# Products without a reader in TensorE's waits of the last group, and a slot table worked out in two parts

## The chip, the cores and the metric

One NeuronCore of a Trainium2 chip runs the whole kernel in one launch. The metric is the device time of one execution in microseconds. The trace covers the span from the first to the last instruction; the time of an execution is about 2 us longer than its span.

## The reference

Two transformer layers over 16 sequences of 128 tokens, width 192, 12 heads of 16, all in float32. Cut to what matters here:

```python
h = tok_embed(x, itok)                       # two gathered tables, layer norm, gate
h = h + L0_attn(layernorm(h))                # linear attention with cumulative sums
h = h + L0_ffn(layernorm(h))                 # 15% of tokens attend, the rest mix; then gelu(n2 @ W1) @ W2
h = h + L1_attn(layernorm(h))                # softmax attention: exp(q k^T), 12 heads per sequence
h = h + L1_ffn(layernorm(h))                 # 8 experts, the two best of each token, gelu MLP 192-768-192
```

The last line is routed: each token has two experts, and the kernel sorts the 4096 (token, expert) pairs into tiles of 128 rows that belong to one expert each. There can be up to 39 such tiles (`MT`).

## The kernel before

The 16 sequences go through in four groups of four (`G = 4`, `NG = 4`). Every engine has its program written out by hand in one order, and the engines meet only in semaphores: `w(turn, name, n)` waits until `n` steps of the stage `name` are done. TensorE works strictly in the order written.

`front(0)` does the first layer of group 0. `joint(g + 1, g)` weaves the first layer of one group with the second layer of the group before, so TensorE has two chains to draw from. `back(NG - 1)` is what is left: feed-forward, second attention and routing of the last group alone. In it TensorE has one chain only:

- the norm `ln4` (VectorE, a root on GpSimd), `n4_T` (TensorE transposes into PSUM), an evacuation on ScalarE, and then the products of `up_half`, `down_half`, `qk1_half`, `v1_half`;
- the second attention, sequence by sequence (b = 0 to 3): `logits(b)`, then VectorE's `maxima(b)`, `max_T(b)` (three transposes), VectorE's `below(b)`, `logits_T(b)`, ScalarE's `exps(b)`, `av1(b)`, `o_T(b)`, VectorE's `attend(b)`. With `wide` the even sequences live in the four PSUM banks `QC` and the odd ones in `QA`, and `logits(b)` waits for the second step of `attend(b - 2)`;
- the expert tiles. `work(k)` on TensorE is `up(k + 1)`, `x_T(k + 2)`, `down(k - 1)`. VectorE's `evacuate(k)` copies the transposed tile k + 2 (`xT_evac`), copies its expert's weights (`stage_w1`) and scales the output of tile k - 1 (`weight`). GpSimd's `add(k)` adds the 128 rows to the output by an indirect DMA; each add waits until the one before has landed. SyncE's `slot_load(k)` fetches a tile's rows, and from tile 6 on waits for the add of tile k - 6.

Which expert a tile belongs to comes from a table in SBUF. It is worked out twice on VectorE: `table(0, EARLY, NG - 1)` for the first 12 tiles from the groups before the last, and `table(EARLY, MT, NG)` for the other 27 once the last group is routed. The second is called after `evacuate(5)` and `rows_out`, in front of `evacuate(6)`. SyncE sends the last group's rows out (`base_rows(NG - 1)`, behind `rows_out`) in its queue between the slot loads of tiles 9 and 10.

`front` already has a helper `stream(n)`: n products of 32 output rows by 512 columns into a bank that nobody reads.

Of the kernel before, what the change touches and what calls it, by code (L numbers as in the profile page):

```python
# [33 lines left out]
RING = 6  # L34
# [40 lines left out]
def build(nc, a, out):  # L75
    with ExitStack() as ctx:
# [959 lines left out]
        def _(dve):  # L1036
# [448 lines left out]
            def maxima(tb, b, hf, wide=False):  # L1485
                w(tb, "lg1", b + 1)
                nc.vector.reduce_max(mx1[:, :, HD].rearrange("p (j i) -> p i j", i=4)[:, 2 * hf:2 * hf + 2, :],  # L1487
                                     sec(b, wide)[:, 2 * hf:2 * hf + 2, 0:384].rearrange("p i (j t) -> p i j t", j=3), AX.X)\
                    .then_inc(s["mx1"], 1)
# [251 lines left out]
            def back(tb):  # L1741
                ln4_half(tb, 0)
                selected_in(tb, 1)
                ln4_half(tb, 1)
                ln4_half_apply(tb, 0)
                ln4_half_apply(tb, 1)
                ffn_out(tb, 0)
                ln5_half(tb, 0)
                ln5_half_apply(tb, 0)
                ffn_out(tb, 1)  # L1750
                ln5_half(tb, 1)
                ln5_half_apply(tb, 1)
                table(0, EARLY, NG - 1)
                maxima(tb, 0, 0, True)
                maxima(tb, 0, 1, True)
                below(tb, 0, True)
                maxima(tb, 1, 0, True)
                maxima(tb, 1, 1, True)
                below(tb, 1, True)
                attend(tb, 0, True)  # L1760
                maxima(tb, 2, 0, True)
                maxima(tb, 2, 1, True)
                below(tb, 2, True)
                attend(tb, 1, True)
                maxima(tb, 3, 0, True)
                maxima(tb, 3, 1, True)
                below(tb, 3, True)
                dve.wait_ge(ld_w1, 16 * NE)
                stage_w1(0, 0)
                attend(tb, 2, True)  # L1770
                xT_evac(0, 0)
                xT_evac(1, 1)
                stage_w1(1, 1)
                attend(tb, 3, True)
                ln6_stats(tb)
                stage_w1(2, 2)
                ln6_apply(tb)
                xT_evac(2, 2)
                evacuate(1, 1, 0)
                gate_max(tb)  # L1780
                evacuate(2, 2, 0)
                top_two(tb)
                top_weights(tb)
                evacuate(3, 3, 0)
                slot_rows(tb)
                evacuate(4, 4, 0)
                evacuate(5, 5, 0)
                rows_out(tb, 0)
                rows_out(tb, 1)
                table(EARLY, MT, NG)  # L1790
                for tile in range(RING, EARLY):
                    evacuate(tile, tile % RING, tile // RING)

            done = [0]
# [7 lines left out]
                dve.wait_ge(route, n)  # L1802

            def table(lo, hi, g):
                m = hi - lo
                dve.wait_ge(s["pos"], g * PER["pos"])
                n = r_step(STT(cnt[:, 0, :], con("iota8"), -float(REGION), first_row[:, 0, :], ALU.mult, ALU.add))
                r_wait(n)
                n = r_step(TS(cnt_i[:, 0, :], cnt[:, 0, :], 127.0 if lo else 0.0, None, ALU.add))
                r_wait(n)  # L1810
                n = r_step(TS(cnt_i[:, 1, :], cnt_i[:, 0, :], 7, None, ALU.logical_shift_right))
                r_wait(n)
                n = r_step(nc.vector.tensor_copy(cnt[:, 1, :], cnt_i[:, 1, :]))
                r_wait(n)
                if lo:
                    n = r_step(T(cnt[:, 1, :], cnt[:, 1, :], taken[:, 0:NE], ALU.subtract))
                    r_wait(n)
                n = r_step(T(upto, con("le8").rearrange("p (e k) -> p e k", e=NE), bc(cnt[:, 1, :], 1, NE), ALU.mult))
                k = r_step(TS(cnt[:, 3, :], cnt[:, 1, :], -128.0, float(REGION), ALU.mult, ALU.add))
                r_wait(n)  # L1820
                n = r_step(nc.vector.reduce_sum(cnt[:, 2, :], upto, AX.X))
                r_wait(n)
                if lo:
                    r_wait(k)
                    k = r_step(STT(cnt[:, 4, :], taken_d, 128.0, cnt[:, 3, :], ALU.mult, ALU.add))
                    n = r_step(TS(cnt[:, 2, :], cnt[:, 2, :], float(lo), None, ALU.add))
                    r_wait(n)
                else:
                    r_step(fill(upto_e[:, 0:1], 0.0))
                    n = r_step(TS(upto_e[:, 1:NE + 1], cnt[:, 2, :], float(hi), None, ALU.min))  # L1830
                    r_wait(n)
                    r_step(fill(taken[:, NE:NE + 1], 0.0))
                    n = r_step(T(taken[:, 0:NE], upto_e[:, 1:NE + 1], upto_e[:, 0:NE], ALU.subtract))
                    r_wait(n)
                    r_step(T(taken_d, taken[:, 1:NE + 1], taken[:, 0:NE], ALU.subtract))
                    r_step(TS(shift, taken[:, 0:1], 128.0, -128.0 * hi, ALU.mult, ALU.add))
                    r_wait(k)
                    k = r_step(nc.vector.tensor_copy(cnt[:, 4, :], cnt[:, 3, :]))
                at_slot = con("slot")[:, lo:hi]
                n = r_step(T(owner[:, lo:hi, :], bc(at_slot, 2, NE), bc(cnt[:, 2, :], 1, m), ALU.is_ge))  # L1840
                r_wait(k)
                r_wait(n)
                k = r_step(T(skip[:, lo:hi, :], owner[:, lo:hi, :], bc(cnt[:, 4, :], 1, m), ALU.mult))
                n = r_step(nc.vector.reduce_sum(ownf[:, lo:hi], owner[:, lo:hi, :], AX.X))
                r_wait(k)
                k = r_step(nc.vector.reduce_sum(rowf[:, lo:hi], skip[:, lo:hi, :], AX.X))
                r_wait(n)
                n = r_step(TS(own_i[:, lo:hi], ownf[:, lo:hi], float(NE - 1), None, ALU.min))
                r_wait(k)
                k = r_step(STT(skip[:, lo:hi, 0], at_slot, 128.0, rowf[:, lo:hi], ALU.mult, ALU.add))  # L1850
                r_wait(k)
                if lo:
                    k = r_step(T(skip[:, lo:hi, 0], skip[:, lo:hi, 0], shift.to_broadcast([128, m]), ALU.add))
                    r_wait(k)
                k = r_step(TS(skip[:, lo:hi, 1], skip[:, lo:hi, 0], float(NE * REGION), None, ALU.min))
                r_wait(k)
                k = r_step(nc.vector.tensor_copy(row_i[:, lo:hi], skip[:, lo:hi, 1]))
                r_wait(k)
                r_wait(n)
                n = r_step(fill(first[:, 0:1], 0.0))  # L1860
                assert n == (R_DONE if lo else R_EARLY), n
# [17 lines left out]
            def evacuate(tile, u, turn):  # L1879

                if more(tile, 2):
                    xT_evac(tile + 2, (u + 2) % RING)
                    stage_w1(tile + 2, (u + 2) % RING)
                if more(tile, -1):
                    weight(tile - 1, (u - 1) % RING)
# [10 lines left out]
        def _(pe):  # L1896
# [355 lines left out]
            def stream(n):  # L2252
                for _ in range(n):
                    mm(PC[0:32, 0, :], ident[:, 0:32], w_l0[:, 0, 0:512])

            def front(ta):
                stream(4)
                x1_T(ta, 0)
# [184 lines left out]
                attn(ta, 1)  # L2443

            def back(tb):
                n4_T(tb, 0)
                up_half(tb, 0, 0)
                up_half(tb, 1, 0)
                n4_T(tb, 1)
# [18 lines left out]
                    qk1_half(tb, n, 1)  # L2468
                v1_half(tb, 1)
                logits(tb, 0, True)  # L2470
                max_T(tb, 0, True)
                logits_T(tb, 0, True)
                logits(tb, 1, True)
                av1(tb, 0, True)
                max_T(tb, 1, True)
                logits_T(tb, 1, True)
                o_T(tb, 0, True)
                logits(tb, 2, True)
                av1(tb, 1, True)
                max_T(tb, 2, True)  # L2480
                logits_T(tb, 2, True)
                o_T(tb, 1, True)
                logits(tb, 3, True)
                av1(tb, 2, True)
                max_T(tb, 3, True)
                logits_T(tb, 3, True)
                o_T(tb, 2, True)
                av1(tb, 3, True)
                w(tb, "h_l1", 3 * 2 + 2)
                x_T(0, 0, 1)  # L2490
                o_T(tb, 3, True)
                x_T(1, 1, 1)
                w(tb, "h_l1", 3 * 3 + 2)
                pe.wait_ge(route, R_EARLY)
                up(0, 0)
# [172 lines left out]
```

## Time and profile before

| | us |
|---|---|
| median of 3 runs | 879.14 (877.9 to 880.11) |
| the profiled execution | 878.32 |
| its span | 876.3 |
| TensorE busy | 729.2 (83%) |
| VectorE busy | 520.1 (59%) |
| mean granted TensorE clock | 0.923 of full |

The profiled execution lies 0.8 us under the median and 2.0 us over its own span. [...] A float32 product is two instructions, a transpose is one.

### The profile page before, as it was taken

What the parts mean: (1) busy time and instruction counts of PE and PEld (TensorE: products, weight loads), DVE (VectorE), ACT (ScalarE), POOL (GpSimd) and SP (SyncE); (2) the same over time, 40 slices, a digit from 0 to 9 for tenths busy, and PEclk for the clock granted to TensorE, in tenths of its full rate; (3) what the DMA queues carried; (4) which work ended last, traced back from release to release, by engine and by line L of the source; (5) the groups of instructions that cost most, each with busy time, mean ns of one, the idle gap of its engine ahead of it and who ended that gap; (6) DMA issues with size and microseconds to landing.
All of it is one profiled execution on the core that took longest, in us unless ns stands there. A gap on an engine that the chain in (4) does not pass through costs nothing.

```text
span 876.3 us, 15714 instructions
## 1 busy us (share of the span) xinstructions
PE 729.2 (83%) x5548; PEld 561.7 (64%) x5549; DVE 520.1 (59%) x1766; ACT 303.9 (35%) x700; POOL 243.4 (28%) x302
## 2 busy tenths in 40 slices
PE   1888777989678998867899976868878989999993
PEld 0546465566457565656666555757756989998892
DVE  7558757873678785668877476891434553333330
ACT  0033232624333263433244344223323433333330
POOL 5332200460013246001443300142000453333332
PEclk9999989999978999998899997797956999999998
DMA  7960000000000000000122000019301233222220
GB/s 251 411 247 1 1 1 1 19 8 1 1 1 28 27 19 8 1 2 1 37 35 9 1 3 1 1 55 344 90 1 29 43 73 47 38 37 38 36 35 8
DMA packets 29894, 43.63 MB, mean 50 GB/s; under 512 B 5355, under 2 KB 24597, under 8 KB 29830
## 3 DMA queue, kind: packets, MB, share of 16 engines
q1 hardware_dynamic: 19250, 30.87, 10.2%
q0 software_dynamic: 8752, 9.07, 6.5%
q10 hardware_dynamic: 1828, 2.84, 0.9%
q8 instruction: 39, 0.64, 0.3%
q14 instruction: 25, 0.20, 0.1%
HBM read 21.36 MB, written 22.09 MB: 50 GB/s over the span
## 4 chain that ended last, share of the span: by engine, by line
PE 59%; DVE 21%; issue 5%; ACT 5%; DMA 4%; POOL 4%; ACTq 1%; SPq 1%; POOLq 0%; DVEq 0%
PE qa L1898 26%; PE qc L1898 24%; PE qa L1901 4%; PE qc L1901 4%; DMA out<-qk_T 3%; DVE mx L1487 2%; POOL arena_w L438 1%; DVE st L1058 1%; ACT big L814 1%; DVE ctxT L1442 1%; DMA mu_row<-in_mu 1%; DVE qk_T L1493 1%; DVE arena_b L1425 1%; ACTq L641 1%; DVE arena_e L1299 1%
## 5 line engine op out<-in xcount | busy, mean ns | idle before, releaser
L1898 PE MATMUL qc<-arena_w,big 128*128 x468 | 82.8, 327 | 1.4 <-DVE qk_T L1877 1.4
L1898 PEld LDWEIGHTS qc<-arena_w,big 128*128 128x128 f32 x468 | 75.1, 190 | 2.1 <-issue 2.0
L1898 PE MATMUL qa<-arena_b 128*128 128x128 f32 (+2 forms) x688 | 73.1, 287 | 2.9 <-DVE att L1503 2.1
L1898 PEld LDWEIGHTS qa<-arena_b 128*128 128x128 f32 (+2 forms) x688 | 64.5, 191 | 11.5 <-DVE att L1503 2.5
L1898 PE MATMUL qa<-arena_e,nT 128*128 128x192 f32 (+2 forms) x256 | 69.9, 429 | 1.1 <-DVE ga L1369 0.7
L1024 ACT ACTIVATE big<-qa,arena_b 128x128 f32<-128x128 f32 x156 | 43.1, 375 | 74.9 <-PE qc L1898 68.4
L611 POOL DMA_INDIRECT out<-qk_T x39 | 61.0, 1565 | 20.6 <-issue 11.1
L1866 DVE COPY arena_b<-qc 128x256 f32<-128x256 f32 x39 | 16.6, 426 | 81.3 <-PE qc L1901 81.3
L1898 PEld LDWEIGHTS qa<-arena_e,nT 128*128 128x128 f32 x256 | 47.2, 200 | 22.9 <-issue 12.9
L474 POOL TENSOR_TENSOR rs_a<-rs_a,minus_half 128x8 f32<-128x8 f32 x4 | 6.6, 1644 | 175.5 <-DVE rs_a L1336 175.5
L1898 PE MATMUL qc<-qk_T 32*128 32x128 f32 (+1 forms) x680 | 33.5, 321 | 17.9 <-DVE qk_T L1493 13.5
L1901 PE MATMUL qa<-cst,arena_b 128*128 128x128 f32 (+2 forms) x232 | 35.5, 297 | 10.8 <-DVE arena_e L1299 5.3
L1898 PEld LDWEIGHTS qc<-qk_T 32*128 32x128 f32 (+1 forms) x680 | 27.1, 214 | 25.3 <-DVE qk_T L1493 17.1
L1487 DVE TENSOR_REDUCE mx<-qc 128x6 f32<-128x768 f32 x28 | 25.5, 954 | 28.1 <-PE qc L1898 28.1
L1901 PEld LDWEIGHTS qa<-cst,arena_b 128*128 128x128 f32 (+2 forms) x232 | 28.1, 149 | 20.3 <-issue 11.7
L1898 PE MATMUL qc<-xT,arena_e 128*128 128x512 f32 (+1 forms) x88 | 38.2, 585 | 1.7 <-ACT xT L781 1.7
L706 ACT ACTIVATE arena_e<-qa 128x512 f32<-128x512 f32 x42 | 23.5, 596 | 45.4 <-PE qa L1901 45.3
L814 ACT ACTIVATE big<-qc 128x768 f32<-128x768 f32 x28 | 21.2, 808 | 48.1 <-PE qc L1898 48.1
L1024 ACT ACTIVATE big<-qa,big 128x128 f32<-128x128 f32 x78 | 21.5, 373 | 38.9 <-PE qc L1898 38.9
L536 POOL DMA_INDIRECT slots<-xk,pos_i x32 | 31.8, 995 | 10.3 <-issue 10.3
L1898 PE MATMUL qa<-arena_b,big 128*128 128x128 f32 (+1 forms) x312 | 31.7, 284 | 3.4 <-issue 2.6
L519 POOL TENSOR_TENSOR arena_b<-arena_w,ck 128x576 f32<-128x576 f32 x16 | 18.5, 1164 | 54.2 <-DVE cf L1269 48.2
(390 smaller groups left out, 1598.5 us busy)
## 6 DMA issues: line engine op xcount, KB each, us to landing
slots<-xk SPq DMA_DIRECT2D x1, 13192.0 KB, 41.8
arena_e<-in_w SPq DMA_DIRECT2D x8, 579.0 KB, 8.1
arena_w<-in_w SPq DMA_DIRECT2D x8, 576.0 KB, 9.4
qk_T<-slots SPq DMA_DIRECT2D x39, 97.0 KB, 1.9
out<-hb SPq DMA_DIRECT2D x16, 96.0 KB, 1.7
arena_e<-in_w_l SPq DMA_DIRECT2D x1, 804.0 KB
arena_e<-in_W ACTq DMA_DIRECT2D x1, 768.0 KB
out<-qk_T POOLq DMA_INDIRECT x39, 3.5
```

Source lines behind the costliest of these rows:

```text
L438: pool.indirect_dma_start(out=dst[:, b, :], out_offset=None, in_=a[table], in_offset=bass.IndirectOffsetOnAxis(ap=idx_cur[:, k, b:b + 1], ...
L519: pool.tensor_tensor(qk48[:, b % 2, 1, :, 0:48].rearrange("p h (k d) -> p h k d", k=3), bc(rq[:, b, H:24, :], 2, 3), bc(ck[:, b, :, :], 3, ...
L536: pool.indirect_dma_start(out=slots, out_offset=bass.IndirectOffsetOnAxis(ap=pos_i[:, k, b:b + 1], axis=0), in_=xk[:, k, b, :], in_offset= ...
L611: pool.indirect_dma_start(out=rows_out, out_offset=bass.IndirectOffsetOnAxis(ap=xs[:, u, D + 1:D + 2].bitcast(I32), axis=0), in_=ym[:, u, ...
L641: act.dma_start(dst, src).then_inc(sem, 16)
L706: A(qkTf[:, b % 2, j * 512:(j + 1) * 512], lin(b, wide)[:, j, :], ACT.Copy).then_inc(*done("qk_evac"))
L814: A(eT[:, b % 2, 6 * hf:6 * hf + 6, :].rearrange("p (i j) t -> p i (j t)", i=2), sec(b, wide)[:, 2 * hf:2 * hf + 2, 0:384], ACT.Exp, scale ...
L1024: i = A(hTm[:, u % 2, j, :], PS[u % 2][:, j % 2, j // 2 * 128:j // 2 * 128 + 128], ACT.Gelu, bias=w1s[u % 3][:, F + FJ // 2 * 128 + j:F + ...
L1487: nc.vector.reduce_max(mx1[:, :, HD].rearrange("p (j i) -> p i j", i=4)[:, 2 * hf:2 * hf + 2, :], sec(b, wide)[:, 2 * hf:2 * hf + 2, 0:384 ...
L1866: nc.vector.tensor_copy(xTm[:, u % 2, :, :], PD[:, 0, 0:256].rearrange("p (c t) -> p c t", c=C)).then_inc(m_xTe, 1)
L1898: return nc.tensor.matmul(o, l, r, start=start, stop=stop)
L1901: return nc.tensor.transpose(o, i, ident[0:k, 0:k])
```

## The change

A helper `hold(bank, n)` writes n products of 32 output rows by 256 columns into the first 32 partitions of a PSUM bank. Nobody reads them. 31 calls' worth of them are placed in `back` on TensorE: 9 around `n4_T(tb, 0)`, 18 in the second attention, and 4 in front of the first expert tile. The function `table` is cut: its small first steps stay in `table`, and the steps that are as wide as the tiles go into `table_rows`. The second table is called as `table` in front of `evacuate(5)` and `table_rows` behind it, and `evacuate(6)` now precedes `rows_out`.

```diff
                 table(0, EARLY, NG - 1)
+                table_rows(0, EARLY)
...
                 evacuate(4, 4, 0)
+                table(EARLY, MT, NG)
                 evacuate(5, 5, 0)
+                table_rows(EARLY, MT)
+                evacuate(6, 0, 1)
                 rows_out(tb, 0)
                 rows_out(tb, 1)
-                table(EARLY, MT, NG)
-                for tile in range(RING, EARLY):
+                for tile in range(RING + 1, EARLY):
                     evacuate(tile, tile % RING, tile // RING)
...
+            def table_rows(lo, hi):
+                m = hi - lo
+                r_wait(done[0])
                 at_slot = con("slot")[:, lo:hi]
                 n = r_step(T(owner[:, lo:hi, :], bc(at_slot, 2, NE), bc(cnt[:, 2, :], 1, m), ALU.is_ge))
-                r_wait(k)
                 r_wait(n)
...
+            def hold(bank, n):
+                for _ in range(n):
+                    mm(bank[0:32, 0:256], ident[:, 0:32], w_1q[:, 0, 0:8, :].rearrange("p h d -> p (h d)"))
...
             def back(tb):
+                hold(QC[:, 3, :], 7)
                 n4_T(tb, 0)
+                hold(QC[:, 3, :], 2)
                 up_half(tb, 0, 0)
...
                 logits(tb, 0, True)
+                hold(QA[:, 3, :], 4)
                 max_T(tb, 0, True)
+                hold(QA[:, 3, :], 1)
                 logits_T(tb, 0, True)
                 logits(tb, 1, True)
                 av1(tb, 0, True)
+                hold(QC[:, 3, :], 2)
                 max_T(tb, 1, True)
+                hold(QC[:, 3, :], 1)
                 logits_T(tb, 1, True)
                 o_T(tb, 0, True)
+                hold(QC[:, 3, :], 1)
                 logits(tb, 2, True)
                 av1(tb, 1, True)
+                hold(QA[:, 3, :], 2)
                 max_T(tb, 2, True)
+                hold(QA[:, 3, :], 1)
                 logits_T(tb, 2, True)
                 o_T(tb, 1, True)
+                hold(QA[:, 3, :], 1)
                 logits(tb, 3, True)
                 av1(tb, 2, True)
+                hold(QC[:, 3, :], 2)
                 max_T(tb, 3, True)
+                hold(QC[:, 3, :], 1)
                 logits_T(tb, 3, True)
                 o_T(tb, 2, True)
+                hold(QC[:, 3, :], 2)
                 av1(tb, 3, True)
                 w(tb, "h_l1", 3 * 2 + 2)
                 x_T(0, 0, 1)
                 o_T(tb, 3, True)
                 x_T(1, 1, 1)
+                hold(QC[:, 1, :], 4)
                 w(tb, "h_l1", 3 * 3 + 2)
                 pe.wait_ge(route, R_EARLY)
                 up(0, 0)
```

## Rows read from the trace of the kernel before

**Rows 1.** The page: the span, and the granted clock in 40 slices of 21.9 us.

```profile
span 876.3 us, 15714 instructions
PEclk9999989999978999998899997797956999999998
```

**Rows 2.** Windows: stretch, length, busy us of each engine, granted clock, DMA share, GB/s.

```profile
34.80:38.20 3.40, 3.38 (x4) 0.68 (x5) 1.25 (x4) 0.00 (x0) 0.00 (x0) 0.51 1.04 378
404.00:414.00 10.00, 9.48 (x61) 7.29 (x60) 8.72 (x51) 3.13 (x8) 2.28 (x4) 0.99 0.00 0
591.30:601.50 10.20, 7.16 (x20) 5.49 (x21) 3.37 (x14) 2.40 (x5) 5.76 (x10) 0.50 0.85 322
635.60:673.60 38.00, 29.26 (x317) 21.24 (x317) 16.73 (x40) 9.30 (x13) 1.01 (x1) 0.51 0.07 17
```

**Rows 3.** The chain that ended last, feed-forward stretch: start, us, what.

```profile
595.43 3.78 PE qc L1898 x8
...
600.06 4.22 PE qa L1898 x16
...
606.01 3.45 PE qa L1898 x16
```

**Rows 4.** Timeline of TensorE: start, us, operation, idle time before it and its releaser.

```profile
52.45 3.62 PE L1898 MATMUL qc<-arena_e,cst 128*32 128x512 f32 x8
...
593.24 1.09 PE L1901 MATMUL qc<-cst,xb 128*96 128x128 f32 x4 [3.68 <-DVE xb L1097]
...
617.10 0.60 PE L1901 MATMUL qc<-cst,xb 128*96 128x128 f32 x4
...
711.61 2.44 PE L1898 MATMUL qa<-arena_b,big 128*128 128x128 f32 x24 [2.34 <-issue]
```

**Rows 5.** The chain again, second attention and the first tiles.

```profile
632.90 0.98 PE qc L1898 x24
...
635.79 0.91 PE qc L1901 x3
...
642.22 0.91 PE qa L1901 x3
...
650.59 0.92 PE qc L1901 x3
651.53 0.56 DVE qk_T L1493
652.14 1.66 PE qc L1898 x24
...
655.35 1.71 PE qa L1898 x24
...
658.96 0.91 PE qa L1901 x3
...
663.80 1.48 PE qa L1898 x24
665.35 0.66 PE qc L1901 x2
...
669.42 6.61 PE qa L1898 x48
```

**Rows 6.** Timeline of VectorE around the second table.

```profile
701.14 0.43 DVE L1866 COPY arena_b<-qc 128x256 f32<-128x256 f32 x1 [2.60 <-PE qc L1901]
...
705.12 0.16 DVE L1807 SCALAR_TENSOR_TENSOR arena_b<-cst,first_row 128x8 f32<-128x8 f32 x1
...
707.07 0.38 DVE L1840 TENSOR_TENSOR arena_b<-cst,arena_b 128x216 f32<-128x216 f32 x1
...
709.55 0.43 DVE L1866 COPY arena_b<-qc 128x256 f32<-128x256 f32 x1
```

**Rows 7.** Timeline of GpSimd: the serial adds after the scatters.

```profile
712.78 0.19 POOL L610 TENSOR_TENSOR spare<-minus_half 128x1 f32<-128x1 f32 x1 [2.43 <-DMA out<-qk_T]
...
717.17 0.19 POOL L610 TENSOR_TENSOR spare<-minus_half 128x1 f32<-128x1 f32 x1 [1.86 <-DMA out<-qk_T]
```

**Rows 8.** One window while a slot load runs.

```profile
723.00:724.00 1.00, 1.00 (x11) 0.94 (x8) 0.43 (x1) 0.00 (x0) 0.90 (x1) 1.00 0.44 110
```

More of the change, by code:

```diff
@@ L1804, in table @@
             def table(lo, hi, g):
-                m = hi - lo
                 dve.wait_ge(s["pos"], g * PER["pos"])
@@ L1824, in table @@
                     r_wait(k)
-                    k = r_step(STT(cnt[:, 4, :], taken_d, 128.0, cnt[:, 3, :], ALU.mult, ALU.add))
-                    n = r_step(TS(cnt[:, 2, :], cnt[:, 2, :], float(lo), None, ALU.add))
-                    r_wait(n)
+                    r_step(STT(cnt[:, 4, :], taken_d, 128.0, cnt[:, 3, :], ALU.mult, ALU.add))
+                    r_step(TS(cnt[:, 2, :], cnt[:, 2, :], float(lo), None, ALU.add))
                 else:
@@ L1837, in table @@
                     r_wait(k)
-                    k = r_step(nc.vector.tensor_copy(cnt[:, 4, :], cnt[:, 3, :]))
+                    r_step(nc.vector.tensor_copy(cnt[:, 4, :], cnt[:, 3, :]))
+            def table_rows(lo, hi):
+                m = hi - lo
+                r_wait(done[0])
                 at_slot = con("slot")[:, lo:hi]
                 n = r_step(T(owner[:, lo:hi, :], bc(at_slot, 2, NE), bc(cnt[:, 2, :], 1, m), ALU.is_ge))
-                r_wait(k)
                 r_wait(n)
```

## The prediction

> **What bounds the kernel now.** I read the page first. TensorE is busy 83% of the span, and the row of granted clocks has a hole at slices 29 and 30, a 5 and a 6, in a kernel that otherwise stands near full [rows 1]. These slices are the last group alone. [...] Last comes a hole at full clock: TensorE idles 2.34 us before 711.61 [rows 4], while VectorE works on the second table from 705.12 to 709.55 before it copies the next tile [rows 6].
>
> **Step 1, what one product costs.** The change's shape, 32 outputs by 256 columns, is not in the trace. The nearest are 32 by 512, 8 instructions in 3.62 us at full clock [rows 4], or 0.9 us a product and 0.45 for half the columns, and 128 by 256, 16 instructions or 8 products in 3.45 us [rows 3], 0.43 each. I take 0.43; at half clock twice that, 0.86. Both shapes agree, so the bounds are 0.43 and 0.47.
>
> **Step 2, norm and first products.** Seven products fill 3.0 us of the 3.68 us wait, two more (0.86) fill the wait for ScalarE's evacuation, which is 595.43 less the end of the transposes at 594.33, 1.1 us [rows 3, 4]. Nothing waits for them as long as the clock is full. If it stays full, the first transposes take 0.60 instead of 1.09 [rows 4], saving 0.5. Eight instructions take 3.78 at half clock and half of 3.45 at full, 1.73: saving 2.05 [rows 3]. Four transposes, 600.06 less 599.21, are 0.85 now and about 0.44 at full: 0.4. Sixteen instructions, 4.22 against 3.45: 0.77. Sum **3.7 us**. Behind this TensorE is bound by itself at full clock either way, and ScalarE's gelus follow it. If the clock were at half, seven products would take 6.0 us, 2.3 more than the wait.
>
> **Step 3, second attention.** The steady cycle, one sequence, is 650.59 to 658.96, 8.37 us: three transposes 0.92, `below` 0.56, `logits_T` 1.66, then to 655.35 another 1.55 (three transposes 0.85 and 0.7 of `attend` on VectorE), `logits` 1.71, and 1.90 of maxima and handing over [rows 5]. At full clock the transposes are 0.5 (three of the four in 0.60), `logits` 0.98, `logits_T` 0.9 since the next follows it. The cycle becomes 0.5 + 0.6 + 0.95 + 0.45 + 0.7 + 0.98 + 1.9 = 6.1, a saving of 2.3. The single product behind `max_T` hides in `below` (0.43 in 0.6), the one behind `o_T` in `attend` (0.43 in 0.7), and `av1` (about 0.85) with two products (0.86) in the maxima (1.9), margin 0.2. Two such cycles: 4.6. From `max_T(0)` to `max_T(1)` it is 6.43 now [rows 5]. There `logits(1)` runs early, and `av1(0)` waits for 1.6 us of exponentials (663.80 less 662.2, which is 658.96 plus the 3.2 from 650.59 to the end of `logits_T`), so products reach past the maxima: 0.5 + 0.6 + 0.95 + 1.6 + 0.85 + 0.86 = 5.4, where without the two products it would be 4.9. That is 1.0 saved and 0.5 given up. The four products before `max_T(0)` are 1.72 in a wait of 1.9: nothing. `max_T(3)` to the end of `logits_T(3)`, 3.2 now, is 2.1: 1.1 saved. Sum **6.7 us**.
>
> From there the first tile's rows are the next thing late: its transposes start at 665.35, 3.15 us after the logits that free the buffer [rows 5], and `av1(3)` ended 0.07 before. With `av1` and its exponentials done 2.5 us after the logits, the load sets the start, so `av1`'s faster clock is worth nothing; the two products before it (0.86 in 1.2) cost nothing. The shorter transposes up to `x_T(1)` give 0.4. The last four products (1.72) hide in VectorE's staging, some 2.1 us from the end of `x_T(1)` near 667.3 to 669.42 [rows 5]. Then 48 instructions in 6.61 us [rows 5] would take twice 2.3 to 2.4 [rows 4], 4.7: 1.9 saved. Sum **2.3 us**.
>
> **Step 4, the table.** Its two parts are 707.07 - 705.12 = 1.95 us and 709.55 - 707.07 = 2.48 us [rows 6]. The first goes before `evacuate(5)`, where VectorE idles 2.60 us before 701.14 [rows 6]: covered. The second follows `evacuate(5)`, ends at about 706.1, and the tile that VectorE then needs is transposed near 707.3 (TensorE's idle time begins at 709.27, and `down(5)`, about 1.95 us, comes before it): covered, 1.2 to spare. `rows_out` goes behind `weight(5)` and also lies in an idle stretch. So TensorE's 2.34 us goes: **2.3 us**, nothing if the adds are the bound instead. Of what queues behind: SyncE's base rows now leave near 711, and the slot load of tile 10 behind them waits for an add that lands after 712 anyhow, since add 5 is released at 712.78 [rows 7]. `table_rows(0, EARLY)` is the same instructions at the same place. The one added wait is for steps already done.
>
> **Sum.** 3.7 + 6.7 + 2.3 + 2.3 = 15.0 us off the span of 876.3 [rows 1], 861.3. The profiled execution was 2.0 us over its span and 0.8 under the median, so **864 us**.
>
> **Rivals.**
>
> [...]
> *The table gives nothing.* The adds are serial, 4.39 us apart [rows 7], against some 4.6 of a tile on TensorE (2.44 + transposes + down); being 2.3 us ahead, a slot load that waits for an add could come late. At 723 to 724 the load of tile 12 is running [rows 8], and its transposes are due near 727.6, so 3.6 us of slack exist and 1.3 stay. And the adds catch up by 0.2 a tile over 30 tiles. If it fails: **866 us**.
>
> **How the numbers follow.** Clock full in both stretches and the table won: 0.62, 862.5 to 866. The table alone fails: 0.08, 866. Dips: 0.20, 866 to 873. Held at half in the attention or lost in more than three cycles: 0.10, 876 to 883. The range 861 to 873 takes the first three with the products' bounds (31 x 0.04 = 1.2, if nothing hid it) and leaves out the last. Within 0.3% (2.6 us) is what a measurement cannot tell from no change: 0.04; slower 0.06; faster 0.90.
>
> **What would show it.** The clock row without its hole; `max_T(1)` to `max_T(2)` 6.1 us; transposes of n4 at 0.6; `max_T(1)` released by a product's end and not by VectorE; no idle 2.34 before `up(8)`; adds after the scatters chained by their own DMA for longer. A row with clock 0.5 between logits and the first tile, or a hold product longer than 0.47 us, would make it wrong.

## The result, and the profile after

The changed kernel takes **865.17 us** (median of 4 runs, 864.49 to 867.48) against 879.62 of the kernel before on the same chip (4 runs, 877.9 to 880.21): a ratio of 0.9844, 95% interval 0.9819 to 0.9868. Ratios here and below leave out runs over 1.5% above the fastest of their kernel and are not quotients of the medians beside them. The forecast was 864 in 861 to 873. The profiled run is the slowest of the four, 867.48 with a span of 865.7, so its stages are compared, and not its total.

The page of the kernel after: span, TensorE, and the granted clock in 40 slices of 21.6 us.

```profile
span 865.7 us, 15836 instructions
PE 732.4 (85%) x5610; PEld 558.5 (65%) x5611; DVE 519.0 (60%) x1766; ACT 303.5 (35%) x700; POOL 248.3 (29%) x302
PEclk9899978999967999999799998789999999999998
```

The 7 of slice 27 and the 5 and the 6 of slices 29 and 30 in [rows 1] are gone; the digits below 9 that are left lie ahead of the last group (slices 1, 5, 6, 11, 12, 19 and 24 to 26, counted from 0 as there), but for the very last. The windows over the two stretches of the last group in [rows 2], 591.3 to 601.5 and 635.6 to 673.6, and the one between (stretch, length, busy us of PE, PEld, DVE, ACT and POOL, granted clock, DMA share, GB/s), kernel after:

```profile
591.30:601.50 10.20, 9.53 (x48) 6.13 (x47) 6.04 (x28) 2.26 (x5) 5.94 (x10) 1.00 0.70 244
601.50:635.60 34.10, 32.63 (x190) 28.61 (x189) 10.17 (x51) 14.42 (x31) 1.50 (x3) 1.00 0.66 217
635.60:673.60 38.00, 34.22 (x433) 24.17 (x433) 19.57 (x46) 14.22 (x30) 2.26 (x5) 1.00 0.07 17
```

The granted clock is 1.00 where it was 0.50 and 0.51. Before, each of the two stretches lay behind a wait of TensorE, 3.68 us for the norm [rows 4] and 1.91 for VectorE's maxima (635.79 less the end of the logits at 633.88, [rows 5]), and the second lasted into the 48 instructions of 669.42 (0.50 from 669 to 673, 0.99 from 673 to 680). TensorE's groups are on the chain that ended last in both [rows 3, 5]. TensorE is busy 34.22 of 38 us instead of 29.26, part of it with products nobody reads, and more of the kernel fits into the same window. TensorE's timeline in the kernel after (start, us, operation, idle time before it and its releaser) answers to [rows 4, 5]; `128*32` marks the new products, two instructions each (the first line's x14 are seven of them; a transpose is one, the 28 of run 6 are x28):

```profile
592.44 3.21 PE L1902 MATMUL qc<-w_1q,cst 128*32 128x256 f32 x14
596.20 0.71 PE L1905 MATMUL qc<-cst,xb 128*96 128x128 f32 x4 [0.55 <-DVE xb L1097]
596.85 1.05 PE L1902 MATMUL qc<-w_1q,cst 128*32 128x256 f32 x4
598.02 1.99 PE L1902 MATMUL qc<-xT,arena_e 128*128 128x256 f32 x8
...
639.18 0.85 PE L1902 MATMUL qc<-big,v 128*17 128x128 f32 x24 [0.96 <-ACT big L814]
639.85 1.03 PE L1902 MATMUL qc<-w_1q,cst 128*32 128x256 f32 x4
640.81 0.55 PE L1905 MATMUL qa<-cst,mx 128*128 128x128 f32 x3
647.04 0.55 PE L1905 MATMUL qc<-cst,mx 128*128 128x128 f32 x3 [0.32 <-DVE mx L1487]
653.27 0.55 PE L1905 MATMUL qa<-cst,mx 128*128 128x128 f32 x3 [0.32 <-DVE mx L1487]
658.60 0.41 PE L1905 MATMUL qc<-cst,qk_T 128*128 128x128 f32 x2 [0.70 <-DMA qk_T<-slots]
662.20 4.88 PE L1902 MATMUL qa<-arena_b 128*128 128x128 f32 x48 [0.29 <-DVE att L1503]
698.19 2.12 PE L1902 MATMUL qc<-arena_w,big 128*128 x12
700.19 2.44 PE L1902 MATMUL qa<-arena_b,big 128*128 128x128 f32 x24
```

Seven products fill 592.44 to 595.65, and 0.55 us of the 3.68 wait is left. The transposes of `max_T(1)` at 640.81 have no idle time before them and follow a product; those of `max_T(2)` and `max_T(3)` wait 0.32 us for VectorE's maxima, so the products before them fit. The first tile at 658.60 waits for its load. `up(8)` at 700.19 follows `down` without the 2.34 us of [rows 4].

From the end of the last joint stage's output products (589.55 before, 592.51 after):

| stretch | before | after | forecast saving | measured |
|---|---|---|---|---|
| wait for the norm | 3.69 | 3.69 | 0 | 0 |
| first n4 transposes to `logits(0)` | 39.66 | 36.32 | 3.7 | 3.34 |
| `logits(0)` to `max_T(0)` | 2.89 | 2.89 | 0 | 0 |
| `max_T(0)` to `max_T(1)` | 6.43 | 5.40 | 1.0 | 1.03 |
| two cycles to `max_T(3)` | 16.74 | 12.46 | 4.6 | 4.28 |
| `max_T(3)` to `x_T(0)` | 6.39 | 5.33 | 1.1 | 1.06 |
| `x_T(0)` to `up(0)` | 4.07 | 3.60 | 0.4 | 0.47 |
| `up(0)` to `up(2)` | 7.69 | 5.95 | 1.9 | 1.74 |
| `up(2)` to `up(8)` | 34.50 | 32.04 | 2.3 | 2.46 |
| `up(8)` to the end | 164.69 | 165.51 | 0 | -0.82 |
| sum | 286.75 | 273.19 | 15.0 | 13.56 |

The change doesn't touch what lies ahead of this table; there this execution was 2.96 us slower than the profiled one before, which leaves 10.6 between the spans.

VectorE's timeline around the second table, kernel after, answers to [rows 6]:

```profile
692.18 0.43 DVE L1870 COPY arena_b<-qc 128x256 f32<-128x256 f32 x1 [0.84 <-PE qc L1905]
...
694.47 0.37 DVE L1845 TENSOR_TENSOR arena_b<-cst,arena_b 128x216 f32<-128x216 f32 x1
...
698.39 0.43 DVE L1870 COPY arena_b<-qc 128x256 f32<-128x256 f32 x1 [1.32 <-PE qc L1905]
```

The table's second part starts at 694.47, behind `evacuate(5)`, and is over by 697.07, and the next copy still waits 1.32 us for TensorE's transposes: 1.32 to spare, where 1.2 was forecast. GpSimd's serial adds, kernel after, answer to [rows 7]:

```profile
713.17 0.19 POOL L610 TENSOR_TENSOR spare<-minus_half 128x1 f32<-128x1 f32 x1 [2.18 <-DMA out<-qk_T]
...
717.72 0.19 POOL L610 TENSOR_TENSOR spare<-minus_half 128x1 f32<-128x1 f32 x1 [2.10 <-DMA out<-qk_T]
```

They are 4.55 us apart here, and no idle time of TensorE is put down to them. They stay released by their own DMA up to the add at 772.08, where in the kernel before VectorE's output was first the later one at 735.25: chained for longer, as forecast.

### The profile page after: what moved, and what is told of

The parts are those of the page before. It is cut to its first block, busy times and chain, and to the rows that moved or that the text cites. A ratio compares the mean times of both kernels' runs of the same rounds, so it can differ in the third digit from the quotient of the medians.

```text
span 865.7 us, 15836 instructions
## 1 busy us (share of the span) xinstructions
PE 732.4 (85%) x5610; PEld 558.5 (65%) x5611; DVE 519.0 (60%) x1766; ACT 303.5 (35%) x700; POOL 248.3 (29%) x302
## 4 chain that ended last, share of the span: by engine, by line
PE 60%; DVE 20%; issue 5%; ACT 4%; DMA 4%; POOL 4%; ACTq 1%; SPq 1%; POOLq 0%; DVEq 0%
PE qa L1902 27%; PE qc L1902 25%; PE qa L1905 4%; PE qc L1905 4%; DMA out<-qk_T 3%; DVE mx L1487 2%; POOL arena_w L438 1%; DVE st L1058 1%; ACT big L814 1%; DMA mu_row<-in_mu 1%; DVE ctxT L1442 1%; DVE arena_e L1299 1%; DVE qk_T L1493 1%; DVE arena_b L1425 1%; ACTq L641 1%
## 5 line engine op out<-in xcount | busy, mean ns | idle before, releaser
L611 POOL DMA_INDIRECT out<-qk_T x39 | 64.3, 1649 | 19.8 <-issue 10.1
L1902 PE MATMUL qc<-qk_T 32*128 32x128 f32 (+1 forms) x680 | 31.0, 304 | 16.2 <-DVE qk_T L1493 12.1
L1902 PEld LDWEIGHTS qc<-qk_T 32*128 32x128 f32 (+1 forms) x680 | 25.2, 199 | 23.9 <-DVE qk_T L1493 16.2
L1902 PE MATMUL qc<-xT,arena_e 128*128 128x512 f32 (+1 forms) x88 | 36.4, 562 | 0.7 <-ACT xT L781 0.6
L610 POOL TENSOR_TENSOR spare<-minus_half 128x1 f32<-128x1 f32 x39 | 8.6, 220 | 85.0 <-DVE qk_T L1881 45.0
```

The costliest lines, as they stand in the source:

```text
L611: pool.indirect_dma_start(out=rows_out, out_offset=bass.IndirectOffsetOnAxis(ap=xs[:, u, D + 1:D + 2].bitcast(I32), axis=0), in_=ym[:, u, ...
L1902: return nc.tensor.matmul(o, l, r, start=start, stop=stop)
```

## The experiments

Twelve runs on three chips, labelled A, B and C here; the chip of the result above is called the first chip. The kernel before took 883.11 us on A (median of 24 runs; a 25th of 2386.01 is left out; 871.94 to 886.04), 885.17 on B (882.46 to 889.68) and 884.6 on C (883.45 to 889.24). Each time is compared with its own chip's. The full change was run on B alone (run 5), so on A and C runs are set beside it by stages. "From the attention's end" means the stretch that the table above sums.

**1. Products alone** (chip A): the change without its edits to the table.

```python
# TensorE: every hold(...) of the change; VectorE as before:
                evacuate(5, 5, 0)
                rows_out(tb, 0)
                rows_out(tb, 1)
                table(EARLY, MT, NG)
```

> The 31 products alone, the table as before. If the two parts of the change add up, this is the whole change less the 2.3 us of TensorE's idle time before up(8): 867.5 us, granted clock full from 589 to the tiles, and the idle 2.34 us before up(8) still there. Rival: the adds are the bound in the tile stage, so that the table is worth nothing once the products have brought the tiles forward: then this run is 865, like the whole change.

Measured 875.91 (868.98 to 877.84, 10 runs), ratio 0.9953 [0.9905, 1.0]; the profiled run, 868.98, is its fastest. The median lies 7.2 us under the kernel before of this chip, where 12.1 was forecast for the first chip (879.6 less 867.5), and 12.1 lies outside the interval too. Each stage from n4 to `up(2)` is that of the full change within 0.1 us, so the products do there what they do in the full change. But `up(2)` to `up(8)` is 39.13 us, with idle time before two tiles. Timeline of TensorE, this kernel:

```profile
689.90 3.96 PE L1898 MATMUL qa<-arena_b 128*128 128x128 f32 x24 [1.35 <-issue]
...
700.23 4.04 PE L1898 MATMUL qa<-arena_b,big 128*128 128x128 f32 x24 [4.02 <-issue]
```

That is 4.6 us more than the 34.50 before, and 3.2 more than the 35.93 of run 3 on this chip, which has the table's edit: the stage shows more than the table's own hole here (run 5). The attention's end comes at 585.38 here and at 591.88 to 592.89 in the other three profiles from this chip, with the same code ahead of it: the stretch ahead varies by some 7 us by itself.

**2. Table alone** (chip A): every `hold(...)` line left out.

> The table in two parts alone, no product. If it is worth TensorE's 2.34 us of idle time: 877.3 us. If the serial adds or a slot load take it back: 879.6 and an idle time of TensorE before a later tile's transposes. The two clock holes stay in both.

Measured 878.04 (872.83 to 883.91, 10 runs), 0.9976 [0.9934, 1.0019]: 5.1 us under the kernel before by the medians, but the interval holds no change as well as the 2.3 us forecast. Windows of this kernel, columns as above:

```profile
596.60:603.00 6.40, 5.30 (x16) 3.93 (x17) 1.52 (x3) 1.01 (x2) 5.04 (x9) 0.50 1.00 400
637.00:645.80 8.80, 5.76 (x78) 4.30 (x78) 4.10 (x6) 2.00 (x3) 0.00 (x0) 0.61 0.00 0
645.80:661.00 15.20, 8.84 (x183) 6.49 (x183) 8.55 (x17) 5.43 (x8) 0.00 (x0) 1.00 0.01 2
661.00:671.00 10.00, 7.37 (x55) 5.93 (x55) 5.36 (x21) 1.86 (x3) 1.01 (x1) 0.52 0.24 61
```

I had not foreseen this. The clock falls ahead of the same two places (n4 to `logits(0)` takes 38.97 us, where the table above has 39.66 and 36.32), but it comes back by itself for 15 us with TensorE busy only 8.84 of 15.20: the two cycles are 6.23 and 6.24 us with no product in them. Then it falls once more. So what products are worth in the attention is not one number: with none there, the clock stayed down in both profiles of the kernel before and came back in runs 2 and 9, whose instructions in that stretch are the same. Within run 2 the granted clock of the whole span ranges from 0.911 (883.91 us) to 0.938 (872.83), so executions of one kernel differ too, though only one was profiled.

**3. Without the single products** (chip A). There are six of them in the attention; the recorded text below counts seven.

```diff
-                hold(QA[:, 3, :], 1)
                 logits_T(tb, 0, True)
 ... and the five others of one product
```

> The whole change without the 7 single products behind max_T and o_T; those in twos and fours stay. If the twos and fours alone hold the clock: no change, 865 us, cycles of 6.1 to 6.2 us. If the singles are needed: the clock falls to half inside the attention, and a cycle there becomes 8.4 plus the overhang of the two products, 1.3, so 867 for one dip to 875 for all cycles.

Measured 871.48 (870.25 to 872.0, 10 runs), 0.989 [0.9855, 0.9925]. The window of this kernel:

```profile
590.00:680.00 90.00, 80.74 (x716) 64.83 (x713) 39.06 (x135) 34.60 (x72) 11.38 (x18) 1.00 0.37 119
```

The clock is full, and every stage up to `up(2)` is that of the full change within 0.1 us; `up(2)` to `up(8)` is 35.93, beside 35.99 in run 5. The singles bring nothing. Runs 1 to 3 also show how the parts add up on this chip, by the medians: products alone 7.2 us, table alone 5.1, both (without singles) 11.6.

**4. The attention with its six singles only** (chip A): its groups of two and four left out, 12 products; the nine around n4 and the four before the first tile stay, 19 in all.

> The whole change with only the 7 single products in the attention; the four before max_T(0) and the twos are gone, those at the norm and before the first tile stay. By my theory the wait of 1.9 us for the maxima, bare, costs the clock as before: half clock from max_T(0), 7.9 us of gain gone, 873 us. Rival: the clock needs little and the singles do, then the 0.5 us overhang before max_T(1) is saved and it is 864.7.

Measured 871.4 (865.95 to 872.06, 4 runs), 0.9883 [0.9796, 0.9971]. Windows of this kernel:

```profile
636.70:640.00 3.30, 2.97 (x56) 2.23 (x52) 1.56 (x2) 1.51 (x2) 0.00 (x0) 0.50 0.00 0
640.00:673.00 33.00, 27.50 (x344) 20.19 (x340) 17.47 (x44) 12.64 (x28) 2.19 (x5) 1.00 0.08 20
```

The clock fell for 3.3 us between `max_T(0)` and `max_T(1)`, which took 5.54 us instead of 5.40, and stood full after that. I had expected half clock from `max_T(0)` on and 873 us; after those 3.3 us there was none of it. One of the four executions, 865.95, lies 4.9 us under the next; it was not profiled.

**5. The full change again** (chip B).

> The changed kernel once more, beside the runs below on their chip. In the run alone it was 865.2 against 879.6 before. If TensorE's extra stall of 3 to 4 us near tiles 6 to 8, which the four runs so far showed and this kernel's first profile did not, comes with the chip and not with the edits, it shows here too: up(2) to up(8) 36 us and not 32, and a time near 869.

Measured 871.5 (870.79 to 872.46, 4 runs), 0.9836 [0.9792, 0.9879]: the ratio of the first measurement, with both kernels some 6 us higher than on the first chip. All stages but one repeat within 0.1 us. `up(2)` to `up(8)` is 35.99 instead of 32.04. TensorE's timeline and the windows around it, this kernel:

```profile
698.64 3.53 PE L1902 MATMUL qa<-arena_b 128*128 128x128 f32 x24 [2.26 <-issue]
```

```profile
690.00:699.70 9.70, 7.44 (x59) 6.69 (x57) 3.06 (x13) 2.09 (x7) 7.68 (x9) 1.00 0.36 85
699.70:703.20 3.50, 3.50 (x22) 3.05 (x21) 2.61 (x12) 1.66 (x6) 2.95 (x3) 0.51 0.17 57
703.20:712.00 8.80, 8.80 (x73) 7.88 (x71) 4.23 (x10) 3.32 (x12) 3.25 (x5) 1.00 0.44 90
```

TensorE waits 2.26 us and behind the wait runs 3.5 us at half clock. The same stage is 35.83 to 36.83 us in all ten kernels with the table's edit that ran on these three chips, run 2 without any product among them, and 39.13 and 40.75 in the two without the edit. So the products don't cause it. In eleven of these twelve profiles (all but run 1) VectorE's wait there ends 0.04 to 0.98 us after the sixth of GpSimd's eight scatters starts, here at 696.67 and 696.89; why is not known.

**6. Transposes in place of products** (chip B): four transposes of the identity for each product, 124 for 31.

```diff
             def hold(bank, n):
-                for _ in range(n):
-                    mm(bank[0:32, 0:256], ident[:, 0:32], w_1q...)
+                for _ in range(4 * n):
+                    tr(bank[:, 0:128], ident, 128)
```

> Each product without a reader is replaced by four transposes of the identity into the same bank, which take the same 0.43 to 0.45 us at full clock. If it matters only that TensorE is busy in the waits: as the changed kernel, full clock from the norm to the tiles, cycles of 6.2 us. If transposes don't count as work for the clock: the clock falls in the wait before n4 or in the attention as it did before, the fillers then take 0.86 at half clock and stick out, and the time is 875 to 885, near the kernel before or above it.

Measured 870.93 (870.25 to 871.68, 4 runs), 0.9835 [0.9792, 0.9878], beside 871.5 of run 5 on this chip. TensorE's timeline and the windows of this kernel:

```profile
591.07 3.28 PE L1905 MATMUL qc<-cst 128*128 128x128 f32 x28
594.82 0.71 PE L1905 MATMUL qc<-cst,xb 128*96 128x128 f32 x4 [0.48 <-DVE xb L1097]
```

```profile
590.00:635.00 45.00, 42.87 (x266) 38.27 (x265) 16.21 (x78) 16.61 (x35) 7.44 (x12) 1.00 0.64 218
635.00:673.00 38.00, 33.58 (x469) 28.82 (x469) 19.20 (x46) 14.88 (x33) 2.34 (x6) 1.00 0.07 18
```

28 transposes in 3.28 us (0.47 for four, where 0.43 to 0.45 was expected) do what seven products in 3.21 do. What fills the wait doesn't matter here, only that it is filled: the transposes kept a clock that was full when they began (whether they would raise one at half is not shown). The recorded text's case that transposes don't count as work for the clock is out for these f32 transposes: with them alone as filling it is 1.00 from 590 to 673, where 0.50 and 0.51 stood in [rows 2].

**7. The products carried on into the joint stages** (chip B): thirteen more in each of three stages.

```diff
+                hold(QA[:, 2, :], 3)
                 av1(tb, 2)
+                hold(QA[:, 2, :], 2)
                 o_T(tb, 2)
...
                 max_T(tb, 3)
+                hold(QC[:, 3, :], 6)
                 logits_T(tb, 3)
...
                 select(ta)
+                hold(QC[:, 3, :], 2)
                 queries(ta)
```

> The changed kernel with 13 more products in each of the three joint stages: 3 before av1(tb, 2), 2 before o_T(tb, 2), 6 between max_T(tb, 3) and logits_T(tb, 3), 2 between select and queries, where TensorE waits 1.6, 1.0, 2.9 and 0.9 us and the clock was at half for some 20 us of each joint. If the clock is held there too and TensorE is on the chain: 1 to 1.5 us for each of nine dips, 855 us. If VectorE sets the pace of the joint stages: the clock rises and the time stays within 2 us of the changed kernel. If the fillers delay what follows: slower by up to 3 x 1.5 us.

Measured 867.13 (866.31 to 868.63, 4 runs), 0.9794 [0.975, 0.9839]: 4.4 us under run 5, with no overlap of the four times each, and far from the 855 that the recorded text has for TensorE on the chain throughout. The attention's end comes at 586.68 instead of 593.28; the granted clock of the whole span is 0.958 against 0.935. As run 1 reached 585.38 without these products, the gain rests on the medians (here, and run 11 beside run 8) and not on this one profile.

**8. Lean** (chip B): no singles, and none before `max_T(1)`, where they reached past the maxima; 23 products are left (the recorded texts of runs 8 and 11 say 22).

> The changed kernel without the 7 single products and without the two before max_T(1), 22 products left. By the working of the prediction the two before max_T(1) stick out by 0.5 us, so max_T(0) to max_T(1) becomes 4.9 and not 5.4 us, and the time falls by 0.5. If the clock falls for want of them: 5.5 and more, and a cycle at half clock with its products sticking out, 2 to 4 us slower.

Measured 871.55 (871.32 to 873.08, 4 runs), 0.9844 [0.98, 0.9888]. `max_T(0)` to `max_T(1)` is 4.77 instead of 5.41, so the overhang of 0.6 is real; but `up(2)` to `up(8)` is 36.48 instead of 35.99, and the total is that of run 5: the forecast fall of 0.5 us did not show. The clock is 1.00 from 590 to 680.

**9. Only the nine around n4** (chip C): all 22 of the attention and the first tiles left out.

> The changed kernel with only the 9 products around n4_T; none in the attention and none before the first tile. The table alone let the clock fall at 637.8 and 661 and rise between, at 645.8; the kernel before had it at half for 38 us. If the attention's products carry their part of the gain (8.6 us in the prediction's sum): the clock falls at max_T(0) and at the latest at the first tile, and the time is 875 to 880 on a chip where the changed kernel takes 871.5. If most executions recover by themselves: 873 to 875, with a wider spread.

Measured 874.75 (869.52 to 875.45, 4 runs), 0.9858 [0.9809, 0.9906]. Windows of this kernel:

```profile
634.00:642.00 8.00, 5.88 (x78) 4.30 (x78) 3.30 (x5) 2.00 (x3) 0.00 (x0) 0.57 0.00 0
642.00:655.00 13.00, 7.49 (x160) 5.50 (x160) 7.05 (x13) 4.01 (x6) 0.00 (x0) 1.00 0.01 3
655.00:662.00 7.00, 5.83 (x58) 3.70 (x58) 2.38 (x6) 3.29 (x4) 0.00 (x0) 0.52 0.17 43
```

n4 to `logits(0)` is 36.32, all of that part's saving. In the attention the clock falls, returns for the two cycles (6.23, 6.24) and falls again, as in run 2. From the attention's end it is 281.47 us, against 276.98 of run 11 on this chip: there the attention's and first tiles' products were worth 4.5 us, not the 8.6 of the table above. The time lies between the two that were forecast, 875 to 880 and 873 to 875.

**10. The products in the attention doubled** (chip C): 18 there become 36, so 31 become 49.

> The changed kernel with every product of the attention twice, 36 there instead of 18. At 0.43 us each the first four become 8, 3.4 us in a wait of 1.9 (+1.5); in a steady cycle two behind max_T 0.86 in 0.6 (+0.2), two behind o_T 0.86 in 0.7 (+0.1), four behind av1 1.72 with 0.2 of cover left (+0.7): cycle 7.2; before max_T(1) +0.9; before av1(3) +0.7. Sum 5 to 5.5 us slower than the changed kernel. Less than 2 would say that products without a reader are cheaper than their 0.43 us and that waits are longer than I read them.

Measured 876.21 (874.17 to 877.55, 4 runs), 0.9886 [0.9847, 0.9925]. That is 4.7 over run 5 on chip B, whose kernel before was 0.6 slower; 5 to 5.5 was forecast. TensorE's timeline of this kernel, the products before `max_T(0)` and then three starts of `max_T`:

```profile
632.15 3.64 PE L1902 MATMUL qa<-w_1q,cst 128*32 128x256 f32 x16
...
642.25 0.55 PE L1905 MATMUL qa<-cst,mx 128*128 128x128 f32 x3
...
649.41 0.55 PE L1905 MATMUL qc<-cst,mx 128*128 128x128 f32 x3
...
656.58 0.55 PE L1905 MATMUL qa<-cst,mx 128*128 128x128 f32 x3
```

Eight products take 3.64 us, 0.455 each. The wait before `max_T(0)` grows by 1.57 (4.46 for 2.89) and the cycles are 7.16 and 7.17 instead of 6.23. From the attention's end it is 284.14 us in this execution, 7.0 more than in run 5. Before `max_T(0)` four more products (1.8 us) cost 1.57, so a product beyond the cover is paid nearly in full there; the 18 together are 8.2 us, of the 7.0 that show 1.0 lies behind `up(8)`.

**11. Lean with the joint stages' products** (chip C): the edits of runs 7 and 8 together.

> The lean back (22 products) with the joint stages' 39 products: e9_joint gained 4 us over the changed kernel on its chip, and the lean back cut max_T(0) to max_T(1) by 0.6 without a time to show for it. Expected 867 where the changed kernel takes 871.5; 866.5 if the 0.6 comes through.

Measured **865.0** (863.17 to 866.82, 4 runs), 0.976 [0.9718, 0.9802]: the largest gain of all, though its interval overlaps that of run 7. Page of this kernel:

```profile
PEclk9999989999999899999889999979999999999997
```

**12. The kernel before once more** (chip C, one run).

> One look at the kernel before on the chip of the runs above, for its trace: if the stall of VectorE and TensorE near tiles 6 to 8 belongs to the chip, up(2) to up(8) is 3 to 5 us over the 34.5 of its first profile; if the clock holes move from one execution to the next, a steady cycle of the attention is 6.2 in part of it and 8.4 in the rest.

Measured 887.57, in a range of the same kernel there of 883.45 to 889.24. The half clock lies at the places of [rows 2], 0.54 and 0.51 in the same windows (TensorE busy 28.34 of the second's 38.00 us), and the cycles are 8.37 and 8.36 as in [rows 5]. `up(2)` to `up(8)` is 40.75 instead of 34.50. The second window, and timelines of TensorE and of VectorE, this kernel:

```profile
635.60:673.60 38.00, 28.34 (x308) 20.45 (x310) 16.74 (x40) 9.29 (x13) 0.91 (x1) 0.51 0.07 17
```

```profile
707.68 4.03 PE L1898 MATMUL qa<-arena_b 128*128 128x128 f32 x24 [2.24 <-issue]
718.75 3.87 PE L1898 MATMUL qa<-arena_b,big 128*128 128x128 f32 x24 [4.71 <-issue]
```

```profile
705.89 0.42 DVE L1866 COPY arena_b<-qc 128x256 f32<-128x256 f32 x1 [6.46 <-remote]
```

VectorE waits 6.46 us for something the profile can't name ("remote", on a kernel of one core), TensorE waits behind it, and the clock falls: it is 0.57 from 708 to 712 and 0.72 from 718 to 724.

## Why the prediction was right, point by point

**One product** was put at 0.43 us, bounds 0.43 and 0.47. Seven took 3.21, or 0.46 each, and two took 1.05, or 0.52 each: a product of a small group costs more than the upper bound. That is the prediction's own sign of being wrong (a product over 0.47 us), met in the pairs and, with 0.62, in the singles, without a price in the steady cycles: the pairs there end 0.32 us before the maxima, and the cycle is 6.23 without the singles too (run 3).

**Norm and first products**, 3.7 forecast, 3.34 measured. The seven hid, as said, and the clock was full behind them. The 0.36 is in the sizes: the four transposes took 0.71 and not 0.60, and the first eight instructions 1.99 and not 1.73, where the rows I worked from had no idle time before them: the four of 617.10 in [rows 4] had none and these had 0.55 us, and eight more of this kernel, at 603.74 with none, took 1.89. The pair in the wait for ScalarE hid: the eight instructions start at 598.02, 1.11 us after the transposes end. Run 9 shows this part to be the nine products' alone. Beside run 2, where the first half-clock stretch was shorter, they are worth 2.65 (38.97 less 36.32).

**Second attention**, 6.7 forecast, 6.4 measured (1.03 + 4.28 + 1.06). The cycle came out at 6.23 against 6.1, the overhang before `max_T(1)` at 5.40 against 5.4, released by a product's end as foreseen. Run 8 prices the overhang at 0.64, where 0.5 was said. What the prediction did not see is that it compared with one execution of the kernel before. Without products the clock in the attention can come back by itself: the cycles were 6.23 in runs 2 and 9. So 6.7 is what the products are worth where the clock stays down throughout, as in both profiled executions of the kernel before, and that the prediction started from such a profile is luck. The kernel before reached 871.94 to 875.34 in 5 of its 24 runs on chip A. A clock that came back would fit that, but so would a quick stretch ahead (some 7 us in run 1) or a missing wait near tiles 6 to 8 (some 4 us, run 5); none of the five was profiled. Nor does the spread tell: the table alone ranged over 11.1 us and the products alone, with a full clock in the attention in the one profile, over 8.9; with both it was 1.8 (run 3) and 1.7 (run 5), but 6.1 in run 4.

**First tiles**, 2.3 forecast, 2.2 measured (0.47 + 1.74). The load became what is late, as said: `x_T(0)` waits 0.70 us for `qk_T<-slots`. The 48 instructions took 4.88 and not 4.7.

**Table**, 2.3 forecast, 2.46 measured. `up(8)` has no idle time before it, and both parts hide with 1.32 us to spare. On chips A to C the stage holds a second wait, of VectorE, with an unnamed releaser. The edit takes 4.3 us off the stage on C, 40.75 without (run 12) and 36.46 with it (run 11), and the wait stays: 6.46 us without and 5.43 with it.

**Tile stage**, 0 forecast, 0.82 lost. Over the 30 tiles from `up(8)`, 140.73 us became 141.51. Of this 0.48 is in one place, `up(9)` to `up(10)`, 5.02 us instead of 4.54, where TensorE's `down` products show 0.16 of idle time ("issue") ahead of them; the rest I can't place, and no experiment was made on it. It is not the table rival's place: no slot load is waited for there.

**The total.** 14.45 us by the medians on the first chip, 15.0 forecast. The split, 12.7 for the products and 2.3 for the table, holds by stages there (11.9 and 2.5). On chip A, where the tiles' stage has its second wait, the medians give 7.2 and 5.1 for the parts alone, and 11.6 for both without the singles. So the sum is shown for the first chip, and the parts' share in the time depends on the chip.

**The rivals.** The clock's dip and return did not happen between n4 and the first tile in either profile of the full change (in run 5 it fell once later, behind the 2.26 us wait of the tiles); in run 4, which has fewer products, it did, for 3.3 us. That transposes leave a cycle unfilled, as this rival has it, no run shows, and run 6 speaks against it. What made the clock fall at 414 in the kernel before (0.88 from 413 to 414, 0.50 from 414 to 420) is not shown. The 34.8 row, set against the rival, is x4 instructions, two of the four products and not all; the other two fall in 38.2 to 40.2, where the clock was 0.98. The slower side, products that don't hold the clock, has nothing for it. Its price for uncovered products held at full clock: run 10 lost 4.7 us, or 5.3 with its chip's kernel before taken into account. That the table gives nothing fell with the 2.46.

**What stays open.** How few products are enough: the six singles aren't needed (run 3), nor, but for 3.3 us of half clock, are the attention's groups of two and four when the singles stand (run 4), and 23 do as well as 31 (run 8). Why the clock comes back by itself in some profiles isn't known. Nor is the wait near tiles 6 to 8 on chips A to C. It lies where GpSimd issues its indirect scatters, and its releaser is none of the kernel's named queues. The loading of instructions is a guess, but the traces speak against it: within VectorE's wait the two instruction queues move no packet in nine of the twelve profiles, and one packet in each of the other three. No experiment was made on it.

## What to carry to other kernels

Look at the granted clock's row for holes, find the wait ahead of each, and fill it with work whose result nobody reads, sized from a row of the same shape to end just inside the wait: within the cover it cost nothing here (cycles of 6.23 us with the single products and without, run 3), beyond it nearly its full time (1.57 us for 1.8, run 10). Measure such a change over many executions, because the kernel without filling may get its clock back in the one that is profiled (1.00 over 15.20 us in run 2), and stretches that the change doesn't touch vary by as much (some 7 us on chip A, run 1).

## What the hardware showed that was not expected

The clock came back from half to full in a stretch where TensorE was busy only 8.84 of 15.20 us (run 2) and 7.49 of 13.00 us (run 9), while in the same stretch of two profiled executions of the kernel before it stayed at 0.51 with 29.26 and 28.34 of 38.00 busy. Transposes of the identity held it as well as products (run 6). A wait of 2.26 us among full tiles was followed by 3.5 us at 0.51 (run 5). And the same kernel has a stage of 32.04 us on one chip and 35.99 on another, about what its wait of 2.26 us and the 3.5 us at half clock behind it come to (2.26 + 1.75).
